# Logits merged with the base product in passes of 264 and 384 columns, and the mixing bias added on VectorE

## The reference

```python
# layer 0: a mixing of the 32 channels, one matrix a batch row
att = softmax(mlp(cond_128))                       # 64 x 8
mixed = einsum('boi,bih->boh', einsum('bk,koi->boi', att, weight), x) + (att @ bias_k)[:, :, None]
# a feed-forward part of 8 experts, the best 2 by gate
gates = softmax of the top 2 of mixed @ gate_w.T
result = mixed @ base_w.T + base_b
result += 2 * (expert low-rank parts: (mixed @ lora_A.T) weighted by gates) @ lora_B
x = x + result
# layer 1: a grouped convolution of 9 taps over the features, plus a context bias,
# then 4 experts, the best 2, low rank; x = x + the experts' sum
```

## Time and profile before

| | |
|---|---|
| median of 3 runs | 184.35 us (184.05 to 185.23) |
| the profiled execution | 183.59 us |
| its span, first to last instruction | 181.9 us |
| granted TensorE clock, mean | 0.995 of full |
| TensorE, matmuls | busy 174.1 us |
| VectorE | busy 119.4 us |
| ScalarE | busy 84.4 us |
| GpSimd | busy 84.2 us |

### The profile page before, as it was taken

One profiled execution on the slowest core, in us unless ns is written; L12 is line 12 of the kernel. 1 busy time (PEld: TensorE's weight loads), 2 busy tenths in 40 slices (PEclk: granted clock), 3 DMA queues, 4 the chain that ended last, 5 costly groups with the idle time before them and its releaser, 6 DMA issues.

```text
span 181.9 us, 2988 instructions
## 1 busy us (share of the span) xinstructions
PE 174.1 (96%) x1079; PEld 157.9 (87%) x1079; DVE 119.4 (66%) x253; ACT 84.4 (46%) x186; POOL 84.2 (46%) x86
## 2 busy tenths in 40 slices
PE   7999999899999999999999999999999999989990
PEld 7987889798888999998889999988889999988970
DVE  1289796987995435987954336897756734578471
ACT  3786578648244176414351366415134653244021
POOL 8024519960588289830019199530007874434000
PEclk9999999999999999999999999999999999999997
DMA  6999000032001410000041000000140000000336
GB/s 180 305 364 382 22 0 2 5 122 109 0 0 51 146 39 0 4 0 0 0 168 67 0 2 0 4 0 0 62 169 4 2 0 4 0 0 2 115 115 231
DMA packets 6350, 12.15 MB, mean 67 GB/s; under 512 B 704, under 2 KB 1088, under 8 KB 6336
## 3 DMA queue, kind: packets, MB, share of 16 engines
q1 hardware_dynamic: 6192, 11.84, 18.3%
q10 hardware_dynamic: 144, 0.13, 0.3%
HBM read 7.77 MB, written 4.19 MB: 66 GB/s over the span
## 4 chain that ended last, share of the span: by engine, by line
PE 75%; DVE 17%; issue 3%; ACT 3%; POOL 0%; DVEq 0%; POOLq 0%
PE ps L909 18%; PE ps L911 17%; PE ps L910 17%; PE ps L985 5%; PE ps L931 5%; PE ps L902 3%; DVE xs L743 2%; DVE late L653 2%; PE ps L1073 2%; DVE xsl L645 2%; PE ps L946 2%; PE ps L1074 2%; DVE above L649 1%; PE ps L982 1%; DVE base_l L645 1%
## 5 line engine op out<-in xcount | busy, mean ns | idle before, releaser
L909 PE MATMUL ps<-base_h,xTh 128*128 128x512 f32 x64 | 26.1, 408 | 0.3 <-DVE base_l L645 0.3
L911 PE MATMUL ps<-base_h,xTl 128*128 128x512 f32 x64 | 25.2, 394 | 0.0
L910 PE MATMUL ps<-base_l,xTh 128*128 128x512 f32 x64 | 25.2, 394 | 0.0
L325 POOL TENSOR_TENSOR xTl<-xT_s,xTh 128x512 fp32r<-128x512 f32 x12 | 15.0, 1277 | 15.8 <-ACT xTh L409 15.8
L330 POOL TENSOR_TENSOR zl<-outb,zh 128x340 fp32r<-128x340 f32 x15 | 14.6, 974 | 13.7 <-ACT zh L434 13.6
L341 POOL TENSOR_TENSOR x1Tl<-x1T,x1Th 128x512 fp32r<-128x512 f32 x12 | 16.4, 1378 | 8.1 <-DVE lw L673 8.1
L702 DVE TENSOR_TENSOR outb<-ps,s_sb 128x340 f32<-128x340 f32 x16 | 8.2, 511 | 17.9 <-PE ps L911 12.7
L689 DVE SCALAR_TENSOR_TENSOR x1T<-ps,side_s,xT_s 128x512 f32<-128x512 f32 x16 | 12.0, 750 | 11.3 <-PE ps L911 11.3
L985 PEld LDWEIGHTS ps<-mixT,p 128*128 128x128 f32 x128 | 17.0, 191 | 1.4
L985 PE MATMUL ps<-mixT,p 128*128 128x128 f32 x128 | 17.0, 276 | 0.0
L434 ACT ACTIVATE zh<-outb 128x340 fp32r<-128x340 f32 x16 | 7.8, 488 | 17.3 <-DVE outb L702 12.6
(11 more groups left out here) (190 smaller groups left out, 469.1 us busy)
## 6 DMA issues: line engine op xcount, KB each, us to landing
xT_s<-in_xT_dram SPq DMA_DIRECT2D x16, 256.0 KB, 4.3
out_dram<-outb SPq DMA_DIRECT2D x16, 256.0 KB, 2.4
x1T<-in_wT_dram SPq DMA_DIRECT2D x4, 256.0 KB, 6.2
x1T<-in_az_dram SPq DMA_DIRECT2D x1, 680.0 KB, 8.0
outb<-in_tapw_dram SPq DMA_DIRECT2D x1, 576.0 KB, 9.2
lgw_s<-in_lgw_dram SPq DMA_DIRECT2D x1, 272.0 KB, 3.3
x1T<-in_lbT_dram SPq DMA_DIRECT2D x1, 256.0 KB, 8.2
outb<-in_b1T_dram SPq DMA_DIRECT2D x1, 256.0 KB, 9.2
```

The source lines that it names most:

```text
L325: nc.gpsimd.tensor_tensor(xTl[:, c, :], xT_s[:, g % 2, c, :], xTh[:, c, :].bitcast(F32), ALU.subtract).then_inc(x_lo, 1)
L909: nc.tensor.matmul(dst, sh, mh, start=start and c == 0, stop=False)
L910: nc.tensor.matmul(dst, sh, ml, start=False, stop=False)
L911: last = nc.tensor.matmul(dst, sl, mh, start=False, stop=stop and c == n - 1)
```

## The change

In groups 1 to 3 the logit weights are split as base_w is and stand in one array with it, xw_h and xw_l, of 136 + 512 = 648 columns a chunk. x_first makes the first 264 columns (136 of logits and the first 128 of base_w) and x_base the other 384, into the same bank one after the other; ScalarE copies 264 (xa_out) and 384 columns (p0_out) to the common tile xp. Group 0 keeps its float32 logits. Its split x now lies in x1Th and x1Tl, so that group 1's split can be made earlier. The bias is no longer a product in each chunk: the column sums are turned once into sum_w (four products of one column and a copy), bias_row(i) spreads the group's bias row over the partitions with one product, and bias_x on VectorE adds sum_w times it to x in place, ahead of make_x1. Orders on all engines are changed with it.

```diff
+WX = LG + D
+HX = LG + P
-KB = 64 + K0
+KB = 32 + K0
...
-        row_w = sb("row_w", [P, D], F32R)
-        row_b = sb("row_b", [96, TOK], F32R)
+        row_w = sb("row_w", [1, D])
+        sum_w = sb("sum_w", [P, DC])
+        row_b = sb("row_b", [KB, TOK], F32R)
+        xw_h = sb("xw_h", [P, DC, WX], F32R)
+        xw_l = sb("xw_l", [P, DC, WX], F32R)
+        base_h, base_l = xw_h[:, :, LG:WX], xw_l[:, :, LG:WX]
...
+        xp = sb("xp", [P, TG, WX])
+        lgs, p0 = xp[:, :, 0:LG], xp[:, :, LG:WX]
+        def x_parts(g):
+            return (xTh, xTl) if g else (x1Th, x1Tl)
...
             pool.wait_ge(lb_lo, 1)
+            for c in range(DC):
+                x_low(1, c)
...
             bias_rows(1)
-            for c in range(DC):
-                x_low(1, c)
...
+            def xa_out(g, t):
+                act.wait_ge(xa_mm, TG * (g - 1) + t + 1)
+                if t == 0:
+                    act.wait_ge(lw_ok, g)
+                    act.wait_ge(y_mm, DC * (g - 1) + 1)
+                nc.scalar.activation(xp[:, t, 0:HX], ps[:, P0[t], 0:HX], ACT.Copy).then_inc(xa_ok, 1)
...
+            def bias_x(i, c):
+                dve.wait_ge(brow_mm, i + 1)
+                dve.wait_ge(xT_in[i % 2][c], 16 * (i // 2 + 1))
+                dve.wait_ge(x_lo, DC * i + c + 1)
+                if i == 0:
+                    dve.wait_ge(xl_mm, 2)
+                    dve.wait_ge(wsum_ok, 1)
+                nc.vector.scalar_tensor_tensor(out=xT_s[:, i % 2, c, :], in0=ps[:, BROW[i], :], scalar=sum_w[:, c:c + 1],
+                                               in1=xT_s[:, i % 2, c, :], op0=ALU.mult, op1=ALU.add).then_inc(xb_ok, 1)
             def make_x1(i, c):
                 dve.wait_ge(y_mm, DC * i + c + 1)
-                dve.wait_ge(xT_in[i % 2][c], 16 * (i // 2 + 1))
+                dve.wait_ge(xb_ok, DC * i + c + 1)
...
             mix_sum(2, prods[1], TG, TG)
+            dve.wait_ge(wsum_mm, 1)
+            nc.vector.tensor_copy(sum_w[:, :], ps[:, WSUM, 0:DC]).then_inc(wsum_ok, 1)
             mix_half(2, 0)
+            lwT_low(0)
             mix_half(2, 1)
-            dve.wait_ge(suv_lo, 3)
-            make_x1(0, 0)
             mix_half(3, 0)
-            make_x1(0, 1)
             mix_half(3, 1)
-            make_x1(0, 2)
-            make_x1(0, 3)
+            dve.wait_ge(suv_lo, 3)
+            for c in range(DC):
+                bias_x(0, c)
+                make_x1(0, c)
...
             sums(0, 0)
             sums(0, 1)
+            lwT_low(1)
+            bias_x(1, 0)
             sums_low(0, 0)
             sums(0, 2)
             sums_low(0, 1)
             sums(0, 3)
-            lwT_low(1)
+            make_x1(1, 0)
             sums_low(0, 2)
             sums_low(0, 3)
+            for c in range(1, DC):
+                bias_x(1, c)
+                make_x1(1, c)
             for i in range(1, G - 1):
                 p, n = i - 1, i + 1
...
                 route1(p)
+                bias_low(n)
+                mwT_low(p)
                 for t in range(TG):
                     logits(n, t)
-                mwT_low(p)
                 route0(n)
-                bias_low(n)
                 make_out(p, 0)
+                bias_x(n, 0)
                 make_out(p, 1)
+                bias_x(n, 1)
                 lwT_low(n)
                 make_out(p, 2)
+                bias_x(n, 2)
+                bias_x(n, 3)
                 make_out(p, 3)
...
+            def x_first(g, t, chunks=range(DC)):
...
+                hi, lo = x_parts(g)
                 for c in chunks:
                     pe.wait_ge(x_lo, DC * g + c + 1)
+                    last = hi_lo(ps[:, P0[t], 0:HX], [(hi[:, c, cols(t)], lo[:, c, cols(t)])],
+                                 [(xw_h[:, c, 0:HX], xw_l[:, c, 0:HX])], start=c == 0, stop=c == DC - 1)
+                if chunks[-1] == DC - 1:
+                    last.then_inc(xa_mm, 1)
...
+            def bias_row(i):
+                pe.wait_ge(obc_lo, i + 1)
+                if i == 0:
+                    pe.wait_ge(lwT_lo, 1)
+                elif i == 1:
+                    pe.wait_ge(prod_ok, MIX_STEPS[G - 1])
+                else:
+                    pe.wait_ge(mwT_lo, 2 * (i - 1))
+                nc.tensor.matmul(ps[:, BROW[i], :], ones_r[0:KB, :], row_b[:, :], start=True, stop=True).then_inc(brow_mm, 1)
...
-                nc.tensor.matmul(ps[:, Y[c], :], row_w[0:KB, cols(c)], row_b[0:KB, :], start=True, stop=False)
...
+            pe.wait_ge(bsum_ok, 1)
+            for c in range(DC):
+                last = nc.tensor.matmul(ps[:, WSUM, c:c + 1], row_w[0:1, cols(c)], ones[0:1, 0:1], start=True, stop=True)
+            last.then_inc(wsum_mm, 1)
             turn_lw(0)
-            x_logits(1, 0)
-            pe.wait_ge(bsum_lo, 1)
-            x_logits(1, 1)
+            for c in range(DC):
+                for t in range(TG):
+                    x_first(1, t, (c,))
             make_y(0)
+            for t in range(TG):
+                mix_logits(1, t)
             pe.wait_ge(in_az, 16)
-            pe.wait_ge(prod_ok, MIX_STEPS[G - 1])
+            pe.wait_ge(x1_ok, DC)
...
             x_base(1, 2)
-            x_base(1, 3, (0, 1))
             turn_lw(1)
-            x_base(1, 3, (2, 3))
+            x_base(1, 3)
+            bias_row(1)
             for i in range(1, G - 1):
                 p, n = i - 1, i + 1
                 make_y(i)
                 for t in range(TG):
                     project(p, t)
-                x_logits(n, 0)
-                x_logits(n, 1)
+                x_first(n, 0)
+                x_first(n, 1)
                 taps(p)
+                x_first(n, 2)
+                x_first(n, 3)
+                x_base(n, 0)
+                turn_mw(p)
                 for t in range(TG):
                     mix_logits(n, t)
-                x_base(n, 0)
-                x_base(n, 1, (0, 1))
-                turn_mw(p)
-                x_base(n, 1, (2, 3))
-                x_base(n, 2)
-                for c in range(DC):
+                x_base(n, 1)
+                for c in range(DC - 1):
                     experts1(p, c)
-                x_base(n, 3, (0, 1))
+                x_base(n, 2)
+                bias_row(n)
                 turn_lw(n)
-                x_base(n, 3, (2, 3))
+                x_base(n, 3)
+                experts1(p, DC - 1)
```

More of the change, by code:

```diff
@@ L530, in _ @@
             nc.scalar.activation(b1_h[:, :], b1T_s, ACT.Copy).then_inc(b1_hi, 1)
-            for t in range(TG):
-                p0_out(0, t)
-            lwT_high(0)
-            for c in range(DC):
-                x_high(1, c)
-            xl_out(1, 0)
-            xl_out(1, 1)
             for g in range(1, G):
                 mix_place(g)
+            for t in range(TG):
+                xa_out(1, t)
             bias_high(1)
@@ L547, in _ @@
             p0_out(1, 1)
-            sums_high(0, 0)
-            sums_high(0, 1)
             p0_out(1, 2)
@@ L552, in _ @@
             p0_out(1, 3)
-            sums_high(0, 2)
-            sums_high(0, 3)
+            for t in range(TG):
+                sums_high(0, t)
             for i in range(1, G - 1):
@@ L827, in _ @@
             sums(0, 3)
-            lwT_low(1)
+            make_x1(1, 0)
             sums_low(0, 2)
             sums_low(0, 3)
+            for c in range(1, DC):
+                bias_x(1, c)
+                make_x1(1, c)
             for i in range(1, G - 1):
                 p, n = i - 1, i + 1
-                for c in range(DC):
-                    make_x1(i, c)
+                if i > 1:
+                    for c in range(DC):
+                        make_x1(i, c)
                 if i == 1:
@@ L946, in mix_logits @@
+                pe.wait_ge(mix_ok, BT * (i + 1) if i < 2 else BT * G)
                 nc.tensor.matmul(ps[:, LGM[t // 2], lg_cols(t)], mixer(i, t), lgs[:, t, :],
                                  start=True, stop=True).then_inc(lg_mm, 1)
-            def x_base(g, t, chunks=range(DC)):
+            def x_first(g, t, chunks=range(DC)):
+                if chunks[0] == 0:
+                    if g == 1:
+                        pe.wait_ge(p0_ok, t + 1)
+                        pe.wait_ge(lgw_lo, 1)
+                    elif t == 0:
+                        pe.wait_ge(zo_ok, TG * (g - 1) - 1)
+                    elif t == 1:
+                        pe.wait_ge(s_ok, TG * (g - 1))
+                    elif t == 2:
+                        pe.wait_ge(ze_ok, TG * (g - 1))
+                    else:
+                        pe.wait_ge(zo_ok, TG * (g - 1))
+                hi, lo = x_parts(g)
@@ L950, in x_base @@
                 for c in chunks:
                     pe.wait_ge(x_lo, DC * g + c + 1)
+                    last = hi_lo(ps[:, P0[t], 0:HX], [(hi[:, c, cols(t)], lo[:, c, cols(t)])],
+                                 [(xw_h[:, c, 0:HX], xw_l[:, c, 0:HX])], start=c == 0, stop=c == DC - 1)
+                if chunks[-1] == DC - 1:
```

(10 more changed lines are left out.)

174 lines of the change are left out of this document (87 added, 87 removed).

## The result

The changed kernel took 182.09 us (median of 6 runs, 181.69 to 182.84) beside 184.2 us for the kernel before (6 runs, 183.66 to 185.23): ratio 0.9894, 95% interval 0.9861 to 0.9926. Forecast were 182.4 us and -1.9; it is -2.1. The profiled execution took 182.84 us, its span is 181.1. Medians are over runs that lie within 1.5% of the fastest of their kernel; only e3_no_bias_x has a run outside, of 183.99 us, which is left out.

The account below looks back on a forecast made before the run. TensorE's queue was taken as the bound where the change works. Gains of 0.9 us up to project(0, .) and 0.5 in each of groups 2 and 3 made -1.9, so 182.4 us, range 179.6 to 185.2.

Parts of the forecast that it names:

- Prices on TensorE: Products of 264 and 384 columns cost 0.1215 and 0.175 us, by a line of 0.44 ns a column plus about 4 ns.
- term (a): TensorE, groups 1 to 3: logit passes go, 512-column products become 264 and 384; net -0.61 us a group, -1.8 in all.
- Term (b): TensorE, make_y: 16 bias products of 512 columns go, one a group comes at 0.232 us; -2.8 us.
- Term (c): TensorE, behind group 0's products: four one-column products turning the column sums, two passes each, add 0.9 us.
- the walk: Stepping through the make_y stages, engine by engine, to find when each operation starts and where TensorE stalls; gave -1.9 us.
- ScalarE and GpSimd at nothing: Changed copies and splits on ScalarE and reordered subtractions on GpSimd cost 0, since both engines wait; ScalarE at most 0.65 us.
- make_y(1): Starts at 52.5 us, stalls 0.7 and 0.65 before chunks 2 and 3; project(0, .) comes 0.9 us earlier.
- Groups 2 and 3: -0.46 us each, including stall 0.7 and lw 0.15 late; make_y(2) 21.5 us behind P, where projections end.
- A: Rival, whole kernel: TensorE alone decides, no new stall, -4.7 us less the waits of 0.15, time 180.0; chance 0.24.
- B: Rival, make_y(1): VectorE and GpSimd overlap, small operations slow to 1.3 to 1.5 us, time 188.1; chance with D 0.12.
- C: Rival, groups 2 and 3: VectorE comes 1 us later than walked, so no change, 184.4 us; chance 0.14.
- D: Rival, TensorE: a 384-column product costs as much as 512 columns, +8 us, time 190.6; chance 1 in 100.

Follow-up runs that it names:

- e3_no_bias_x: Changed kernel without the 16 bias_x operations on VectorE, so the mixing bias is missing from x1; row products stay: 181.65 us.
- e7_merge_only: Changed kernel with merged logits and new orders kept, but the bias again a 72-row product in each chunk of make_y: 183.83 us.
- e4_split136: Changed kernel with the 648 columns a chunk cut into 136 and 512 instead of 264 and 384: 189.33 us, one run.
- e1_rows72: Changed kernel with the bias row product on 72 rows instead of 40, the added rows zero: 181.27 us.
- e9_low_behind: e2_fullrows with VectorE's sums_low(0,2) and sums_low(0,3) moved behind bias_x(1,1) and make_x1(1,1): 181.44 us.
- e8_more_dve: Changed kernel plus unread VectorE operations of bias_x's form behind bias_x(n, 2), two in group 2 and one in group 3: 182.95 us, one run.
- e6_rows_and_order: e2_fullrows with VectorE's make_y(1) work reordered, most sums later, and ScalarE's x_high(2) ahead of the last two sums_high: 181.01 us.
- e0_changed_again: The changed kernel, unedited, measured and profiled a second time: 181.84 us.
- e2_fullrows: e1_rows72 with the column sums turned by products of 128 rows instead of one: 181.68 us.

## Why the prediction was right

The sum was -1.9 and the measurement is -2.1 (-2.4 by the stretches). The total was right, but two of its terms were off and partly offset each other.

- **Prices on TensorE**: right within about 1%. 264 and 384 columns cost 0.122 and 0.177, which makes term (a) -0.49 a group instead of -0.61, and e7_merge_only shows -0.47 and -0.51. The line was used inside its widths; e4_split136 shows that at 136 columns it fails.
- **Term (b), the bias products**: "one product a group comes", at 0.232. It costs 0.26 to 0.28 more, since it has 40 rows (e1_rows72). Over four groups the term is about -1.7 instead of -2.8. This is the term that was mis-sized most.
- **Term (c), the column sums**: 0.98 for 0.9, right in size. What it costs is another matter: the walk let GpSimd's low parts start at 26.5, and they start 0.04 behind A, which is 27.5 in the clock of before. Without the column sums TensorE waits for them (e7_merge_only: 0.79). That the 0.98 of the column sums covers a start that the walk had 1 us too early is luck.
- **ScalarE and GpSimd at nothing**: right for ScalarE, whose p0_out still waits 14.3 us for TensorE; right for GpSimd only by that cover.
- **make_y(1)**: forecast was that it "starts at 52.5" with stalls of 0.7 and 0.65. Counted from A that start is 25.0; it came at 26.1, half of the delay being the two row products, the rest steps of about 0.1 where the queue changes shape (5.96 instead of 5.83 for the 264-column products, for one). Of the stalls the first is missing and the second is 0.5; e3_no_bias_x puts all of VectorE's cost here at 0.74, where 1.35 was charged. Net -0.38 instead of -0.9.
- **Groups 2 and 3**: forecast -0.46 each, measured -1.05. With the measured prices -0.49 - 0.93 + 0.23 + 0.26 is -0.93; make_y(2) itself got 1.01 shorter (7.35 to 6.34) instead of 0.93. From P to make_y(2) it is 21.65, where 21.5 was forecast and 21.70 was before. The "stall 0.7" and the late lw of 0.15 did not come: I had charged bias_x, lwT_low and make_x1 with their durations, but back to back they start 0.60 to 0.66 apart: the ten operations between the end of lw and that of make_x1(2,0), 90.92 to 97.26, took 6.34 where the walk had 7.0. The row product's 0.26 on TensorE gave cover, too, but was not needed: without it, in e1_rows72, these stretches got shorter by nearly all of it. The earlier trace rows could have said it: make_out was charged at 0.64 there, from two in 1.29, and the same holds for the others.
- **Rivals**: A (no stalls, 180.0) is wrong in make_y(1) and right in groups 2 and 3; with the row products at their true price (4 x 0.26) it gives 181.0. Its sum also took the old stall of make_y(1) as 0.3, where the prediction's own 7.84 less 7.3 is 0.54. B did not come, because GpSimd was done with x1_low at 55.73 and idle until 58.81; e9_low_behind shows its size once they meet. C was nearer than it seems: e8_more_dve leaves 0.2 us, where C needs VectorE 1 us later. D is excluded by the 0.177.

## What to carry to other kernels

Work that is moved from a full TensorE queue to a half-idle VectorE is gained as long as each consumer's deadline holds; walk those deadlines with distances between starts, not with durations. A matmul with few rows in a stream of full ones costs more than its columns say, here 0.26 us; more rows cost nothing, so try padding them. A small piece of work on the full engine can be nearly free where a wait would stand in its place, as the column sums are here (0.09 of 0.98). Before closing a stall of half a microsecond by reordering, look at what the moved operations will run beside: twice here the gain was handed back within the next stretch.

## What was not expected of the hardware

The start of the kernel comes in two lengths. In five of the ten profiled executions of the changed kernel and its variants (after, e1, e3, e4 and e6) A lies at 28.73 or later, in the others at 28.08 or earlier. The same eight passes of 136 columns, ahead of all groups, in the kernel before and then after:

```profile
6.85 1.19 PE L1105 MATMUL ps<-lgw_s,ones 128*128 128x136 f32 x8
7.61 2.18 PE L1180 MATMUL ps<-lgw_s,ones 128*128 128x136 f32 x8
```

| | first clock record | A |
|---|---|---|
| before | 5.83 | 27.49 |
| after | 10.56 | 29.06 |
| e0_changed_again | 4.90 | 27.73 |
| e1_rows72 | 10.18 | 28.79 |
| e2_fullrows | 5.71 | 27.91 |
| e3_no_bias_x | 9.84 | 28.73 |
| e4_split136 | 10.24 | 28.88 |
| e6_rows_and_order | 10.42 | 30.18 |
| e7_merge_only | 4.22 | 28.08 |
| e8_more_dve | 4.54 | 27.66 |
| e9_low_behind | 4.30 | 27.05 |

In all eleven the pace changes at that record: ahead of it products of 256 columns stand 0.213 apart (and those of 136, where they come that early, 0.227), behind it 0.12 and 0.116. So until then TensorE ran at the lower of its two levels, 1.2 GHz. The profile shows it busy without a gap from 1.24 us up to the rise in every one of them, early or late, and what tells the two cases apart is not shown. The late rise moves A of the same kernel by 1.33 us (after against e0_changed_again), over half of what this change brings. It does not explain all of A: e6 also waits 0.80 for a split of the weights. How many of the unprofiled runs behind the medians had the late rise is not on record, which is one more reason to read the stretches behind A.
